# Chunked attention on one core: the scalar engine takes the first eviction of queries or values ahead of the mask's negatives, and the copy of the squares last

## The reference

```python
def _chunk_attn(q, k, v, masks, W_in, b_in, W_out, b_out):   # H = 8 heads, chunks of 64
    qh = proj(q, Wq, bq); kh = proj(k, Wk, bk); vh = proj(v, Wv, bv)
    scores = jnp.einsum('bnqhd,bnkhd->bnhqk', qh, kh) * scale
    scores = scores + jnp.where(km[:, :, None, None, :] > 0, 0.0, NEG)
    attn = jax.nn.softmax(scores, axis=-1)
    out = jnp.einsum('bnhqk,bnkhd->bnqhd', attn, vh).reshape(N, T, C)
    out = out @ W_out.T + b_out
    return out.transpose(0, 2, 1) * masks
out = _chunk_attn(ctx_4096, ctx_4096, ctx_4096, mask, W_in, b_in, W_out, b_out) + x
mu = jnp.mean(out, axis=2, keepdims=True)
var = jnp.mean(jnp.square(out - mu), axis=2, keepdims=True)
return (out - mu) * jax.lax.rsqrt(var + EPS)
```

## Time and profile before

| | before |
|---|---|
| time, median of 3 runs | 2043.45 us (2041.29 to 2044.07) |
| the profiled execution's own time | 2037.81 us |
| its span, first to last instruction | 2036.0 us |
| PE, DVE, ACT, POOL busy | 97%, 88%, 77%, 73% |
| transfers on the hardware queue | 57.2% of 16 engines' span |
| mean granted TensorE clock | 0.993 of full speed |

### The profile page before, as it was taken

One profiled execution on the slowest core, in us unless ns is written; L12 is line 12 of the kernel. 1 busy time (PEld: TensorE's weight loads), 2 busy tenths in 40 slices (PEclk: granted clock), 3 DMA queues, 4 the chain that ended last, 5 costly groups with the idle time before them and its releaser, 6 DMA issues.

```text
span 2036.0 us, 91518 instructions
## 1 busy us (share of the span) xinstructions
PE 1970.8 (97%) x40472; PEld 1595.7 (78%) x40472; DVE 1797.9 (88%) x2181; ACT 1569.9 (77%) x2177; POOL 1496.5 (73%) x1062
## 2 busy tenths in 40 slices
PE   6999999999999999999999999999999999999995
PEld 5787888877777788878778877878878778777883
DVE  4899999989889998999999999998999989898986
ACT  4787787877787777878777887777878778777783
POOL 4677777777777777777777777777777777776774
PEclk9999999999999999999999999999999999999997
DMA  4456666656665556666556555656655566655554
GB/s 156 115 149 171 180 181 180 170 153 175 179 178 162 162 170 177 182 174 174 156 175 187 172 172 170 169 167 189 179 165 160 168 178 177 180 163 158 165 149 144
DMA packets 242890, 342.55 MB, mean 168 GB/s; under 512 B 28992, under 2 KB 94784, under 8 KB 242496
## 3 DMA queue, kind: packets, MB, share of 16 engines
q1 hardware_dynamic: 242496, 336.71, 57.2%
HBM read 168.82 MB, written 67.11 MB: 116 GB/s over the span
## 4 chain that ended last, share of the span: by engine, by line
PE 71%; DVE 8%; ACT 8%; POOL 7%; issue 6%; DMA 0%; ACTq 0%; SPq 0%; POOLq 0%; DVEq 0%
PE proj_bank L291 26%; PE proj_bank L323 15%; PE proj_bank L344 15%; PE o_bank L393 8%; PE score_bank L362 7%; ACT prob_t L465 3%; POOL neg_rows L573 3%; POOL prob L542 2%; POOL ctx_lo L549 2%; DVE row_max L618 2%; DVE squares L641 2%; DVE stats L669 2%; DVE sums L629 2%; ACT score_bank L441 1%; ACT k_f L482 1%
## 5 line engine op out<-in xcount | busy, mean ns | idle before, releaser
L542 POOL TENSOR_TENSOR prob<-prob,recip 128x1024 f32<-128x1024 f32 x256 | 487.8, 1906 | 457.3 <-DVE recip L633 457.3
L618 DVE TENSOR_REDUCE row_max<-score_bank 128x16 f32<-128x1024 f32 x256 | 313.2, 1223 | 168.8 <-PE score_bank L362 168.6
L449 ACT ACTIVATE prob<-prob 128x1024 f32<-128x1024 f32 x256 | 271.5, 1060 | 232.2 <-DVE prob L622 232.2
L549 POOL TENSOR_TENSOR ctx_lo<-ctx_raw,ctx_hi 128x512 fp32r<-128x512 f32 x256 | 332.2, 1298 | 67.3 <-ACT ctx_hi L429 66.2
L291 PE MATMUL proj_bank<-ctx_hi,w_hi 128*128 128x512 f32 x1024 | 347.9, 421 | 6.8 <-ACT v_f L490 5.6
L559 POOL TENSOR_TENSOR y<-y,x_raw 128x512 f32<-128x512 f32 x256 | 325.9, 1295 | 7.5 <-DVE y L660 7.4
L291 PE MATMUL proj_bank<-ctx_lo,w_hi 128*128 128x512 f32 x1024 | 321.9, 396 | 1.0 <-issue 1.0
L622 DVE TENSOR_TENSOR prob<-score_bank,row_max 128x1024 f32<-128x1024 f32 x256 | 313.5, 1225 | 8.8
L291 PE MATMUL proj_bank<-ctx_hi,w_lo 128*128 128x512 f32 x1024 | 319.5, 393 | 1.1 <-issue 1.1
L641 DVE STREAM_TRANSPOSE squares<-prob 128x1024 f32<-128x1024 f32 x256 | 315.9, 1234 | 1.5 <-POOL prob L542 1.5
L629 DVE TENSOR_REDUCE sums<-prob 128x16 f32<-128x1024 f32 x256 | 304.9, 1191 | 2.2 <-ACT prob L449 2.2
(11 more groups left out here) (44 smaller groups left out, 3702.2 us busy)
## 6 DMA issues: line engine op xcount, KB each, us to landing
ctx_raw<-ctx SPq DMA_DIRECT2D x128, 512.0 KB, 6.1
x_raw<-x SPq DMA_DIRECT2D x128, 512.0 KB, 5.1
prob_t<-squares SPq DMA_DIRECT2D x1024, 64.0 KB, 2.5
out<-y SPq DMA_DIRECT2D x128, 512.0 KB, 7.1
mask_all<-mask SPq DMA_DIRECT2D x128, 256.0 KB, 4.3
v_x<-v_f SPq DMA_DIRECT2D x256, 128.0 KB, 3.5
y<-w_in_t SPq DMA_DIRECT2D x1, 768.0 KB, 4.3
y<-w_out_t SPq DMA_DIRECT2D x1, 256.0 KB, 4.2
```

Source lines behind the costliest of these rows:

```text
L542: pool.tensor_tensor(part, part, slots(recip[:, u % 2, :]), ALU.mult).then_inc(norm_done, 1)
L549: pool.tensor_tensor(ctx_lo[:, n % 2, :, tokens], ctx_raw[:, n % BLOCKS, :, tokens], ctx_hi[:, n % 2, :, tokens].bitcast(F32), ALU.subtrac ...
L618: dve.tensor_reduce(row_max[:, :].rearrange("p (r c) -> p r c", c=CPU), rows, AX_X, ALU.max).then_inc(max_done, 1)
```

## The change

In ACT's step the negatives move from in front of the copy of the squares to between the two evictions, and the copy of the squares moves behind both.

```diff
                     high_attention(B, u - 2)
-                    lay_negatives(B, u + 2)
-                    copy_squares(B, u)
+
                     for f in range(HALVES):
                         if h == 0:
                             values(B, j + 1, f)
                         else:
                             queries(B, j + 2, f)
+                        if f == 0:
+                            lay_negatives(B, u + 2)
+                    copy_squares(B, u)
```

## The result

The changed kernel takes 2130.76 us (median of 4 runs, 2129.14 to 2131.81) against 2043.76 before (4 runs by then). The ratio is 1.0421, with a 95% interval of 1.0398 to 1.0444: 87 us slower. The forecast was 2130.5.

A forecast was written before the change was run, and what follows sets the result against it. The kernel was taken as bound by TensorE's own instructions, any delay of the scores paid in full each step. Costs of 102 less 15 saved gave +87 us on the median 2043.45: 2130.5 us, range 2114 to 2148.

The forecast's parts named there:

- the gate's cost: Scores start late in each step because the negatives wait for the first eviction: 0.80 a pair, 127 pairs, 102 us.
- the saving of 15: Earlier evictions end PE's 56 waits for them: between 11.9 and 17 us, taken as 15.
- The odd loop: Odd step, queries' projection through first eviction and negatives to the scores: 3.44 us against 2.98, scores 0.46 late.
- The projection's 1.70: Odd step: time from the projection's start on PE until ACT starts evicting its first half, 1.70 us.
- the eviction's 0.57: Odd step on ACT: time from one eviction of queries to the next instruction, 0.57 us.
- The even loop: Even step, values' projection through first eviction and negatives to the scores: 3.38 us against 3.04, scores 0.34 late.
- the late copy: Copy of the squares on ACT, with SP's four transfers, starts 1.97 us later in the odd step; nothing waits for it.
- The second eviction: On ACT behind the negatives: ends 3.91 us after the projection's start, before its bank is needed; no cost.
- B: Rival: evictions gain and the negatives still come in time, 2028 us, faster; chance 0.03.
- C: Rival: only a part of the gate's cost appears; with half of it 2080 us; chance 0.05.
- A: Rival: some 254 new idle times bring TensorE's clock down, once in a batch 54 us, 2185 us; chance 0.04.
- D: Rival: ACT late with `o_hi`, or PSUM access slowing negatives and DVE; 0.1 us a step gives 2156; chance 0.05.

The follow-up runs named there:

- experiment 1: Against the kernel before: only the copy of the squares moved behind both evictions, the negatives still in front of both; 2026.94 us.
- 11: The kernel of experiment 1 run again, on the same chip as 12; 2028.08 us.
- experiments 5: Against the changed kernel: scores of odd units also wait for the evictions of queries and keys, three waits instead of one; 2176.75 us.
- 9: Against the changed kernel: scores of odd units also wait for the eviction of keys, two waits instead of one; 2152.76 us in a single execution.
- experiments 8: Against experiment 1: the copy of the squares moved between the two evictions, the negatives in front of both; 2020.85 us.
- 12: The kernel with the negatives in front of both evictions and the copy of the squares between them, run again on the same chip as 11; 2020.83 us.
- Experiment 2: Against the changed kernel: the copy of the squares moved directly behind the negatives, before the second eviction; 2125.87 us.
- experiment 7: Against the changed kernel: the negatives moved behind both evictions, then the copy of the squares; 2666.17 us.
- experiment 10: Against the changed kernel: the copy of the squares moved in front of the negatives, both behind the first eviction; 2348.6 us.

## Why the prediction was right

The mechanism was the one named, and the sum came out within 0.3 us of the measured median. Its two parts came out as well, the gate's cost of 102 as 103 or 104 and the saving of 15 as 15.6 and 14.6. But neither part is made of what the prediction put into it, so the last 10 us of agreement are luck.

The gate's cost is the changed kernel against experiments 1 and 11, which differ from it only in the negatives' place: 2130.76 - 2026.94 = 104 and 2130.76 - 2028.08 = 103.

- The odd loop, 3.44 against 2.98: it was 3.37. Two of its terms were a little off. The step from the negatives' end to the scores was read at start-up scores with three waits and applied to scores with one, 0.14 for 0.06; experiments 5 and 9 show that the number of waits makes the difference. The projection's 1.70 and the eviction's 0.57 were 1.71 and 0.58. So 0.39 a step was lost, not 0.46: 49 us in 127 steps, not 58.
- The even loop, 3.38 against 3.04: measured 3.38. Right, 127 x 0.34 = 43.
- Together the loops cost 92 us and not 102. The other 11 or 12 were in no term. PE's idle time without a releaser is 9.0 + 7.6 = 16.6 us in the changed kernel, 9.9 in experiment 1 and 6.1 in 11, which is 7 to 10 of them. The three falls of the clock, 13.6 us at half of full speed where experiments 1 and 11 had none between start-up and end, are worth up to 7 more, an estimate from the rows above.

The saving was reasoned as "at most the waits of PE for evictions", 12 to 17 us. Without the late copy it is 22 (experiments 8 and 12), and the late copy, priced at nothing, takes 6 or 7 of it. These two errors cancel. What was overlooked stood in the list of the kernel before:

```profile
PE proj_bank L323 <- issue: 3.5, 3, 1.9
PE o_bank L393 <- issue: 3.0, 5, 1.3
PE proj_bank L291 <- issue: 3.0, 3, 1.1
PE score_bank L362 <- issue: 2.9, 3, 1.8
```

These 12.4 us are as much as all waits for evictions, 11.9; the prediction said that PE waits for two things only. In experiment 12 they are 3.7, so some 12 + 9 = 21 of its 22 us are accounted for.

Of the smaller forecasts:

- The second eviction was priced at nothing. Experiment 2, where it is later still, bears that out: no wait of PE for it. The late copy was looked for in waits for the transfers, and there it isn't.
- The scores were to start 8.05 and 8.01 us apart; it is 7.97 and 8.00 in the pair shown. PE's share fell to 94%, 93% expected.
- PE was to wait for the negatives about 100 us; the list has 83.9. A wait costs more than its idle time here too, 0.39 for a listed 0.32 and 0.34 for 0.28.
- PE's busy time was not "near 1970" but 1998.9. Part of the 28 us is this unlisted part of the waits, 250 x 0.07 = 18, and part the work at the 1.2 GHz level.

Of the rivals, B was wrong as expected: the first half's end is seen 1.71 after its start, not within 1.24. C fell with the 250 waits and the 92 us. A came only in small in the change, and in earnest in experiment 7. D has two parts. The row of the first eviction shows 0.72 us of idle time in front of it, so `o_hi` was not late. And the negatives take 1.02 us on the mean as before (1.03), DVE's low part of the output 0.63 as before, so no slowing in PSUM shows.

## What to carry to other kernels

Before an instruction is moved behind another, add up the loop that it closes: from the engine that releases the new predecessor, through both instructions, back to the engine that waits, and set that against what this engine has to do in between. Here 3.4 against 3.0 in each step cost 92 us, while evictions in front of the copy but behind the negatives saved 15 to 22. Work that the bound engine waits for at its next instruction goes first; a bank that is needed 0.85 us after that can wait, even when it has been full for long. And when a sum comes out to 0.3 us, check its terms one by one: here two pairs of errors of 7 to 11 us hid in it.

## What the runs showed of the hardware

- Scores with one semaphore to wait for started 0.06 us after the release, with two or three 0.14 (experiments 5 and 9). With one the weight load was released directly; with more a separate wait instruction stood in front of it. In a loop that is closed 127 times this is 11 us.
- Idle gaps of 1.70 us in each step brought TensorE's granted clock to a mean of 0.91 (experiment 7). With gaps of 1.2 to 1.3 us (experiment 10) and of 0.3 us (the change) the mean stayed at 1.00 from 60 to 1760 us. Single gaps of 3.15, 2.35 and 2.08 us in the changed kernel, and of 1.92 before, had a stretch at 0.50 beside them; one of 2.16 at 1718.44 had none.
- Stalls of 0.3 to 3 us inside a row of matmuls, with no semaphore in play, came and went with small edits: in the values' projection 20 times 1.0 us with three waits and 23 times 1.2 with two, all in one step of the batch, and 6 times in the changed kernel. They are worth more than some of the waits that an edit is about.
- These stalls stand beside another thing that the page of the changed kernel lists, packets of 16 KB on a queue called "instruction":

```profile
q8 instruction: 319, 5.23, 1.0%
```

The fourteen traces have 95 stalls of PE of over 0.6 us without a releaser between 60 and 1950 us, and every one of them ends 2.2 to 2.6 us after a packet of q8 starts. Of instants taken at random 6 to 9% do. So it looks as if the matmuls waited for their own instructions to arrive, and as if an edit moved the stalls by moving the places in the program where the next packet is needed. No run changed these packets alone: that they stand together is shown, that one makes the other is not.
